# Expert layer of a two-layer transformer on one Trainium2 core: early down weights, the last two groups of slots added by one-hot products, and the last batch scaled by VectorE

## The chip, the cores and the metric

The kernel runs on one core of a Trainium2 chip. The metric is the device time in microseconds (us) of one execution. The kernel before took 1477.53 us (median of three runs, 1477.40 to 1481.35). Every row below comes from one more execution of it, taken with the profiler; times in rows are microseconds from the start of its span.

## The reference, cut to what matters

Two layers, each an attention and a feed-forward part with a residual and a layer norm behind each. The input is 4 batches of 512 tokens, 256 wide. The change lies in the last part, a mixture of 64 experts:

```python
def _moe_infer(x, gate_w, w_gate, w_up, w_down):      # x: 2048 tokens x 256
    scores = softmax(x @ gate_w.T)                    # 64 experts
    topk_w, topk_i = top_k(scores, 6)
    # each expert takes its first 32 tokens (CAP = 32), in order of token
    g = einsum('ech,ehi->eci', buf, w_gate)           # 256 -> 176
    u = einsum('ech,ehi->eci', buf, w_up)
    y = einsum('eci,eih->ech', silu(g) * u, w_down)   # 176 -> 256
    return (y[flat_i, slot] * (flat_w * valid)[:, None]).reshape(T, K, H).sum(axis=1)
shared = silu(x @ sw_gate) * (x @ sw_up) @ sw_down    # a shared expert, all tokens
x = layernorm(x + moe + shared)
```

All data are fp32.

## The kernel before, in words

Engines run their own instruction lists and meet at semaphores; the order on each engine is written out by hand. Until about 1290 us the kernel does both attentions and the first feed-forward part. Then comes the expert layer:

- Tokens. `rows4` (VectorE) writes the normed rows of batch b to `rows[b]`; ScalarE stores them with their scores to DRAM (`store_rows`), once as `rows_dram` and once, the rows alone, as the start of `sums_dram`. `choose`, `list_tokens`, `merge_lists` pick each expert's 32 tokens (VectorE).
- Groups. 64 experts x 32 slots are 16 groups of 128 slots (4 experts each). GpSimd gathers the 128 rows of each group by an indirect DMA (L717).
- Weights. Each group needs 1408 KB of gate and up weights (`load_hidden`, L460) and 704 KB of down weights (`load_down`, L466, or L1064 from ScalarE's queue for groups 6 to 15). A ring of six buffers holds them (`eg`, `ed`; `RING`). SyncE (SP) issues the loads in order, each behind a wait that says its buffer is free.
- For each group s TensorE does `turn_hidden(s)` (L2266), `gate_up(s + 1)` (L2258), `rows_of(s + 2)` (L2247), `down(s)` (L2275); in some rounds also parts of the shared expert of batches 2 and 3 (`gate_up4`, `down4_products`, L2198). ScalarE copies and scales (`y_in`, L1069); VectorE multiplies (`hidden_rows`, L1641).
- Sums. Two slots of a group, or of the two groups of a pair, can belong to one token. `sum_repeats(h)` adds them by products with 0/1 matrices (`same`, `cross`), VectorE copies the sums out (`summed_rows`, L1645), and GpSimd adds the two groups' rows to `sums_dram` by two accumulating indirect DMAs (L724). A pair's scatters wait for the landing of the pair before, since both may add to one row. Pair 7 is groups 14 and 15.
- End. After all 16 scatters SP loads the sums batch by batch (`fin`, L491). VectorE adds the shared expert's rows (`last_statistics`, L1677) and takes mean and variance (L1407 to L1413), GpSimd the root (`root16`, L636), VectorE the shift (`last_norm`, L1684), ScalarE scales (L1096), SP stores a batch (L495).

## Time and profile before

| | |
|---|---|
| three timed runs | 1477.53 us median, 1477.40 to 1481.35 |
| the profiled execution | 1473.92 us, its span 1472.1 us |
| mean granted TensorE clock | 0.983 |
| busy: TensorE, its weight loads, VectorE, ScalarE, GpSimd | 95%, 76%, 64%, 39%, 38% |
| HBM read and written | 66.22 MB, 9.21 MB |

The profiled execution's 1473.92 us hold the span and 1.82 us around it. Shares of busy time are a mean over stages with different limits; for this change only the last 180 us of the span count, and in them which wait ends last.

### The profile page before, as it was taken

The numbers are of one execution on the slowest core, as the hardware profiler recorded it, in microseconds if no ns is written. First come the engines' busy times: TensorE is split into PE (matmuls) and PEld (weight loads), VectorE is DVE, ScalarE is ACT, GpSimd is POOL, SyncE is SP. The second block draws the span as 40 slices with busy tenths as digits, with TensorE's granted clock in tenths as the row PEclk, the third lists the DMA queues.
The fourth block names the chain that finished last, engine by engine and source line by source line (L and its number), as shares of the span: only waits on it lengthen the run. The fifth ranks groups of instructions, "written<-read, shape, count | busy, mean of one in ns | idle before, by whom it ended". The sixth has DMA issues, their size and how long they took to land.

```text
span 1472.1 us, 23873 instructions
## 1 busy us (share of the span) xinstructions
PE 1396.1 (95%) x8118; PEld 1114.2 (76%) x8118; DVE 934.9 (64%) x2158; ACT 579.7 (39%) x1459; POOL 555.5 (38%) x483
## 2 busy tenths in 40 slices
PE   8999999999999999999999999999999999998990
PEld 7777777777777777777777788888888888875650
DVE  5777777777877777874443457547647647885113
ACT  4444444444444444551221144334334333352322
POOL 3655555555555555400113023513423422204223
PEclk9999999999999999999999999999999999999986
DMA  5000000000002100020000020020020001479984
GB/s 182 1 11 1 12 0 11 0 11 0 11 0 63 11 0 0 14 62 11 1 0 0 1 80 8 12 76 8 9 78 7 7 15 40 126 254 311 277 235 128
DMA packets 68221, 76.39 MB, mean 52 GB/s; under 512 B 14205, under 2 KB 55445, under 8 KB 68149
## 3 DMA queue, kind: packets, MB, share of 16 engines
q1 hardware_dynamic: 56517, 58.36, 13.4%
q10 hardware_dynamic: 8560, 12.36, 2.7%
q0 software_dynamic: 3072, 4.72, 1.6%
q8 instruction: 44, 0.72, 0.2%
q14 instruction: 28, 0.23, 0.0%
HBM read 66.22 MB, written 9.21 MB: 51 GB/s over the span
## 4 chain that ended last, share of the span: by engine, by line
PE 81%; DVE 7%; POOL 4%; ACT 3%; issue 2%; DMA 2%; SPq 1%; POOLq 0%; ACTq 0%; DVEq 0%
PE ps L1699 37%; PE ps L1838 9%; PE ps L1812 7%; PE ps L1800 5%; PE ps L1875 4%; PE ps L1966 4%; PE ps L1805 2%; PE ps L2198 2%; PE ps L2049 2%; PE ps L2258 1%; DMA wo<-in_L_attn_wo_dram 1%; PE ps L2039 1%; PE ps L2275 1%; PE ps L1840 1%; PE ps L1802 1%
## 5 line engine op out<-in xcount | busy, mean ns | idle before, releaser
L808 ACT ACTIVATE probs<-ps,nm 128x128 f32<-128x128 f32 (+3 forms) x256 | 134.0, 526 | 150.1 <-DVE nm L1189 150.1
L650 POOL TENSOR_TENSOR qk<-q,ksb 128x512 f32<-128x512 f32 x64 | 83.5, 1304 | 285.4 <-ACT q L903 212.3
L1838 PE MATMUL ps<-kT,qT 128*128 128x128 f32 (+3 forms) x512 | 174.5, 449 | 4.4 <-ACT probs L808 4.4
L1104 DVE TENSOR_TENSOR pT_low<-ps,pT 128x384 fp32r<-128x384 f32 (+2 forms) x256 | 99.6, 451 | 123.1 <-ACT pT L734 121.9
L1121 DVE TENSOR_TENSOR prod<-ps,rope_sb 128x1024 f32<-128x1024 f32 x128 | 150.2, 1215 | 7.4 <-PE ps L1699 7.4
L734 ACT ACTIVATE pT<-ps 128x384 fp32r<-128x384 f32 (+2 forms) x256 | 84.7, 416 | 152.4 <-PE ps L1875 152.4
L524 POOL TENSOR_TENSOR qT<-prod 64x512 f32<-64x512 f32 x64 | 81.2, 1269 | 167.4 <-DVE prod L1121 128.8
L1812 PE MATMUL ps<-U,oT 128*128 (+1 forms) x512 | 124.5, 386 | 0.0
L524 POOL TENSOR_TENSOR kT<-prod 64x512 f32<-64x512 f32 x64 | 81.4, 1272 | 108.7 <-DVE prod L1121 106.2
L1189 DVE TENSOR_REDUCE nm<-ps 128x1 f32<-128x128 f32 (+3 forms) x256 | 113.6, 484 | 9.3 <-PE ps L1840 9.3
L1246 DVE SCALAR_TENSOR_TENSOR acc<-ps,rinv,acc 128x256 f32<-128x256 f32 x256 | 109.4, 478 | 11.9 <-PE ps L1812 11.9
L1812 PEld LDWEIGHTS ps<-U,oT 128*128 128x128 f32 x512 | 92.4, 190 | 30.9 <-issue 20.9
L1699 PEld LDWEIGHTS ps<-kvo,qn 128*128 128x128 f32 x768 | 100.2, 191 | 8.7 <-DVE qn L1104 4.0
L1699 PE MATMUL ps<-kvo,qn 128*128 128x256 f32 x768 | 102.4, 283 | 2.9 <-DVE qn L1104 2.9
L1699 PE MATMUL ps<-wq,x2T 128*128 128x512 f32 x384 | 99.5, 395 | 5.2 <-POOL wq L582 5.2
L1699 PE MATMUL ps<-xT,wq 128*128 128x512 f32 x384 | 100.1, 408 | 0.5 <-DVE prod L1121 0.5
L1388 DVE SCALAR_TENSOR_TENSOR k<-ps,k 128x512 fp32r<-128x512 f32 x64 | 43.9, 686 | 82.8 <-ACT k L903 82.8
L1838 PEld LDWEIGHTS ps<-kT,qT 128*128 128x128 f32 x512 | 77.4, 190 | 22.6 <-issue 14.2
L1699 PE MATMUL ps<-k,x 128*128 128x512 f32 x384 | 91.6, 394 | 0.2
L1699 PEld LDWEIGHTS ps<-wq,x2T 128*128 128x128 f32 x384 | 72.3, 189 | 21.9 <-issue 4.5
L1699 PEld LDWEIGHTS ps<-xT,wq 128*128 128x128 f32 x384 | 74.2, 194 | 15.0 <-DVE prod L1121 1.3
L1800 PEld LDWEIGHTS ps<-pT,c_tok 128*128 128x128 f32 x384 | 65.6, 188 | 26.1 <-ACT pT_end L734 20.3
(263 smaller groups left out, 2767.9 us busy)
## 6 DMA issues: line engine op xcount, KB each, us to landing
eg<-in_L_ffn_w_gate_dram SPq DMA_DIRECT2D x16, 704.0 KB
eg<-in_L_ffn_w_up_dram SPq DMA_DIRECT2D x16, 704.0 KB
ed<-in_L_ffn_w_down_dram ACTq DMA_DIRECT2D x10, 640.0 KB
ksb<-ks_dram SPq DMA_DIRECT2D x16, 256.0 KB, 3.3
ed<-in_L_ffn_w_down_dram SPq DMA_DIRECT2D x6, 640.0 KB
rows_dram<-rows ACTq DMA_DIRECT2D x4, 640.0 KB, 9.0
acc<-in_L_attn_x_dram SPq DMA_DIRECT2D x4, 512.0 KB
wq_in<-in_L_attn_wq_dram SPq DMA_DIRECT2D x8, 256.0 KB, 2.9
```

The costliest lines, as they stand in the source:

```text
L524: nc.gpsimd.tensor_tensor(dst[0:64, h, b, :], byc[r, 0, :], bys[r, 1, :], ALU.subtract).then_inc(roped, 1)
L650: nc.gpsimd.tensor_tensor(qk[:], q3[:], ksb[b % 2][:], ALU.mult).then_inc(qk_ready, 1)
L734: return nc.scalar.activation(o, i, ACT.Copy)
L808: nc.scalar.activation(probs[hh][:, off:off + (i + 1) * P], ps[:, BS + i % 2, 0:(i + 1) * P], ACT.Exp, bias=nm[:, hh, i:i + 1], accum_out= ...
L1104: return nc.vector.tensor_tensor(o, whole, hi.bitcast(F32), ALU.subtract)
L1121: nc.vector.tensor_tensor(prod[parity][w][:], ps[:, BA:BA + 2, :], rope[:, w:w + 1, :].broadcast_to([P, 2, T]), ALU.mult).then_inc(product ...
L1189: nc.vector.tensor_reduce(nm[:, hh, i:i + 1], ps[:, BS + i % 2, 0:(i + 1) * P], AX_X, ALU.max, negate=True).then_inc(negmax_ready, 1)
L1246: nc.vector.scalar_tensor_tensor(out=a, in0=ps[:, BW + i // 2, (i % 2) * D:(i % 2 + 1) * D], scalar=rinv[:, hh, i:i + 1], in1=a, op0=ALU.m ...
L1699: last = pe.matmul(o, lhs(a), rhs(c), start=start and j == 0, stop=stop and j == 2)
L1800: pe.matmul(ps[:, BO, k * P:T], c_tok[h][:, b * TPB + k, :], pT[:, k, k * P:T], start=k == 0 and h == 0, stop=False)
L1812: last = pe.matmul(ps[:, BW + i // 2, (i % 2) * D:(i % 2 + 1) * D], oT[:, i * P:(i + 1) * P], U[:, bass.ds(2 * g + n % 2, 1), :], start=Tr ...
L1838: pe.matmul(ps[:, bank, 0:(i + 1) * P], qT[:, hh, b, i * P:(i + 1) * P], kT[:, hh, b, 0:(i + 1) * P], start=True, stop=False)
```

## The change

Three things change in the expert layer.

1. Loads. The down weights of groups 3 and 2 are issued right behind group 1's, that of group 2 after a wait for `kvo_ready`. Gate and up weights of groups 2, 3 and 4 follow one another after `out3_ready`; group 4's down weights wait for batch 0's shared gate and up products (`gate4_ready`). To free their places `rows3` and one half of `x3T` of batch 0 lie elsewhere; VectorE's first `match_slots` now waits until `rows3` is stored.
2. Groups 14 and 15 are no longer scattered. GpSimd writes the numbers 0 to 1023 (`tokens`), VectorE compares them with each slot's token and so makes two 0/1 matrices of 128 slots x 2048 tokens (`onehot`), and TensorE multiplies these with the groups' outputs (`y_in`), tile by tile of 128 tokens (`last_rows`), in four pairs of PSUM banks. The shared expert's rows come into the same banks by a product with the identity (batches 1 to 3), or are added by VectorE (batch 0). SP loads the sums after 14 scatters.
3. The last batch is scaled by VectorE (`last_tiles`) and stored in two halves.

```diff
-        x3T ... enumerate(((44, 117), (109, 113), (32, 36), (48, 52)))]
-        rows ... enumerate((61, 56, 104, 85))]
+        x3T ... enumerate(((100, 117), (109, 113), (32, 36), (48, 52)))]
+        rows ... enumerate((61, 56, 104, 40))]
+        onehot = [place(f"onehot{h}", at, [P, TOK]) for h, at in enumerate((32, 76))]
+        tokens = place("tokens", 24, [P, TOK // 2])
+        SCATTERED = GROUPS - 2
+        last_banks = ((5, 6), (0, 1), (3, 4), (2, 7))
...
 # SyncE
             for s in range(2):
                 load_experts(s)
+            load_down(3)
+            sp.wait_ge(kvo_ready, 2 * BLOCKS)
+            load_down(2)
             sp.wait_ge(out3_ready, BLOCKS * PPC)
-            for s in (2, 3):
-                load_experts(s)
+            for s in (2, 3, 4):
+                load_hidden(s)
             sp.wait_ge(sw_lo, 2)
-            wait_rows(sp, 3)
-            load_experts(4)
+            sp.wait_ge(gate4_ready, FT1)
+            load_down(4)
...
-            sp.wait_ge(scattered, 16 * GROUPS)
+            sp.wait_ge(scattered, 16 * SCATTERED)
...
-            for b in range(BATCH):
+            for b in range(BATCH - 1):
                 sp.wait_ge(out_done, TPB * b + TPB)
                 sp.dma_start(out_dram[b], fin[:, b * TPB:(b + 1) * TPB, :]).then_inc(stored, 16)
+            for lo in (0, TPB // 2):
+                hi = lo + TPB // 2
+                sp.wait_ge(last_done, last_done_first + hi)
+                sp.dma_start(out_dram[BATCH - 1][:, lo:hi, :], fin[...]).then_inc(stored, 16)
...
 # GpSimd
-            for s in range(GROUPS):
+            for s in range(SCATTERED):
+                if s == 10:
+                    pool.wait_ge(gate4_ready, BATCH * FT1)
+                    nc.gpsimd.iota(tokens[:], pattern=[[1, TOK // 2]], ...).then_inc(consts4, 1)
...
 # VectorE
             dve.wait_ge(gate4_ready, 2 * FT1)
+            wait_rows(dve, 3)
             match_slots(0)
...
                 if s + 2 < GROUPS:
                     hidden_rows(s + 2)
-            summed_rows(GROUPS // 2 - 1)
+                if s == 12:
+                    dve.wait_ge(consts4, 10)
+                    dve.wait_ge(down4, 2 * BATCH)
+                    link(nc.vector.tensor_scalar(spare[:, 0:2], idxf[:, SCATTERED:GROUPS], float(-(TOK // 2)), None, ALU.add))
+                if s in (12, 13):
+                    h = s - 12
+                    settle()
+                    for half, index in enumerate((idxf[:, s + 2:s + 3], spare[:, h:h + 1])):
+                        nc.vector.tensor_scalar(onehot[h][:, half * (TOK // 2):(half + 1) * (TOK // 2)], tokens[:], index, None,
+                                                ALU.is_equal).then_inc(onehot_ready, 1)
+            def add_sums(b):
+                dve.wait_ge(sums_loaded[b], sums_loaded_first[b] + 16)
+                dve.wait_ge(y_summed, SCATTERED // 2 + b + 1)
+                for j, bank in enumerate(last_banks[b]):
+                    ...  # fin of two tiles += the bank, 128x512
+            def first_sums():     # batch 0: acc += banks, before its sums are loaded
+            def add_first_sums(): # fin += acc
+            def last_tiles():
+                b = BATCH - 1
+                dve.wait_ge(rstd_ready, 13 + b)
+                for t in range(b * TPB, b * TPB + TPB):
+                    nc.vector.tensor_scalar(fin[:, t, :], fin[:, t, :], meanvar16[:, t, 0:1], rstd16[:, t:t + 1],
+                                            ALU.subtract, ALU.mult).then_inc(last_done, 1)
+            first_sums()
+            add_first_sums()
+            statistics16(0, fin)
+            for b in range(1, BATCH):
+                add_sums(b)
+                statistics16(b, fin, lambda: last_shift(b - 1))   # the shift stands amid the four bn_stats
+            last_tiles()
...
 # TensorE
+                if s == GROUPS - 1:
+                    pe.wait_ge(shared_done, 2 * BATCH)
+                    shared_of_second(1)
                 down(s)
...
-            sum_repeats(GROUPS // 2 - 1)
+            def last_rows(b):
+                if b == 0:
+                    pe.wait_ge(hid4_ready, BATCH * FT1)
+                if b == 2:
+                    pe.wait_ge(y_copied, SCATTERED // 2)
+                if b == 0:
+                    pe.wait_ge(onehot_ready, onehot_first + 4)
+                    pe.wait_ge(y_scaled, GROUPS)
+                for i in range(TPB):
+                    o = ps[:, last_banks[b][i // 2], (i % 2) * D:(i % 2 + 1) * D]
+                    t = b * TPB + i
+                    if b >= 2:
+                        pe.matmul(o, ident[:], acc[:, t, :] if b < BATCH - 1 else shared_last[:, i, :], start=True, stop=False)
+                    for h in range(2):
+                        last = pe.matmul(o, onehot[h][:, t * P:(t + 1) * P], y_in[h][:], ...)
+                last.then_inc(y_summed, 1)
+            shared_of_second(0)
+            for b in range(BATCH):
+                last_rows(b)
```

On SyncE's queue, at the loads of groups 1 to 5 (`eg`: gate and up weights of a ring place, `ed`: its down weights), there stood:

```order
L466 DMA ed1<-in_L1_ffn_w_down_dram 8x4x512
L460 DMA eg2<-in_L1_ffn_w_gate_dram 128x4x352 [waits out3_ready]
L460 DMA eg2<-in_L1_ffn_w_up_dram 128x4x352
L466 DMA ed2<-in_L1_ffn_w_down_dram 80x4x512
L466 DMA ed2<-in_L1_ffn_w_down_dram 8x4x512
L460 DMA eg3<-in_L1_ffn_w_gate_dram 128x4x352
L460 DMA eg3<-in_L1_ffn_w_up_dram 128x4x352
L466 DMA ed3<-in_L1_ffn_w_down_dram 80x4x512
L466 DMA ed3<-in_L1_ffn_w_down_dram 8x4x512
L460 DMA eg4<-in_L1_ffn_w_gate_dram 128x4x352 [waits dn_loaded,sw_lo]
L460 DMA eg4<-in_L1_ffn_w_up_dram 128x4x352
```

and there stands now:

```order
L473 DMA ed3<-in_L1_ffn_w_down_dram 80x4x512
L473 DMA ed3<-in_L1_ffn_w_down_dram 8x4x512
L473 DMA ed2<-in_L1_ffn_w_down_dram 80x4x512 [waits kvo_ready]
L473 DMA ed2<-in_L1_ffn_w_down_dram 8x4x512
L467 DMA eg2<-in_L1_ffn_w_gate_dram 128x4x352 [waits out3_ready]
L467 DMA eg2<-in_L1_ffn_w_up_dram 128x4x352
L467 DMA eg3<-in_L1_ffn_w_gate_dram 128x4x352
L467 DMA eg3<-in_L1_ffn_w_up_dram 128x4x352
L467 DMA eg4<-in_L1_ffn_w_gate_dram 128x4x352
L467 DMA eg4<-in_L1_ffn_w_up_dram 128x4x352
L473 DMA ed4<-in_L1_ffn_w_down_dram 80x4x512 [waits gate4_ready,sw_lo]
L473 DMA ed4<-in_L1_ffn_w_down_dram 8x4x512
```

Two groups' down weights moved in front of the wait for `out3_ready`, and group 4's three loads moved from behind the wait for stored rows (`dn_loaded`) to in front of it. Group 5's loads keep their wait for `gate4_ready`.

On VectorE, around the products `hE` of groups 14 and 15 and the copies `xg` of pairs 5, 6 and 7, there stood:

```order
L1645 COPY xg<-ps 128x2x256 [waits y_summed]
L1641 TENSOR_TENSOR hE<-actE,ps 128x176 [waits hE_turned,actE_ready] x2
L1645 COPY xg<-ps 128x2x256 [waits y_summed] x2
L1677 TENSOR_TENSOR fin<-fin,acc 128x1024 [waits shared_done,wd_loaded]
L1407 BN_STATS stat<-fin 128x6 [waits dchain]
```

and there stands now:

```order
L1666 COPY xg<-ps 128x2x256 [waits y_summed]
L1662 TENSOR_TENSOR hE<-actE,ps 128x176 [waits hE_turned,actE_ready]
L1696 TENSOR_SCALAR spare<-idxf 128x2 [waits down4,consts4]
L1701 TENSOR_SCALAR onehot0<-tokens,idxf 128x1024 [waits dchain]
L1701 TENSOR_SCALAR onehot0<-tokens,spare 128x1024
L1662 TENSOR_TENSOR hE<-actE,ps 128x176 [waits hE_turned,actE_ready]
L1701 TENSOR_SCALAR onehot1<-tokens,idxf 128x1024 [waits dchain]
L1701 TENSOR_SCALAR onehot1<-tokens,spare 128x1024
L1666 COPY xg<-ps 128x2x256 [waits y_summed]
L1717 TENSOR_TENSOR acc<-acc,ps 128x512 [waits y_summed]
L1717 TENSOR_TENSOR acc<-acc,ps 128x512
L1723 TENSOR_TENSOR fin<-fin,acc 128x1024 [waits wd_loaded,dchain]
```

The four comparisons stand around the product of group 15 and in front of the copy of pair 6; the copy of pair 7 is gone.

On TensorE, behind the turn of group 15's hidden rows, there stood `down(15)` and the three products of the last pair:

```order
L2275 MATMUL ps<-ed,hET 32x256 [waits y_scaled,hET_ready]
L2275 MATMUL ps<-ed,hET 32x256 x7
L2284 MATMUL ps<-y_in,same 128x256 [waits y_copied,y_scaled]
L2285 MATMUL ps<-y_in,cross 128x256
L2286 MATMUL ps<-y_in,same 128x256
```

and there stands now (the rows for tiles of batches 2 and 3 repeat in the pattern of the last two):

```order
L2357 MATMUL ps<-acc,ident 128x512 [waits hE_ready,shared_done]
L2329 MATMUL ps<-ed,hET 32x256 [waits y_scaled,hET_ready]
L2329 MATMUL ps<-ed,hET 32x256 x7
L2357 MATMUL ps<-acc,ident 128x512 [waits hET_ready,hE_ready]
L2396 MATMUL ps<-y_in,onehot 128x256 [waits y_scaled,gw_turned,hid4_ready]
L2396 MATMUL ps<-y_in,onehot 128x256 x15
L2394 MATMUL ps<-acc,ident 128x256 [waits y_copied]
L2396 MATMUL ps<-y_in,onehot 128x256 x2
```

One product of the identity moved into the gap in front of `down(15)`, another stands behind it, and 40 products of 128x256 follow.

## Rows read from the trace of the kernel before

**Rows 1.** The chain that ended last, from pair 6's copy on: start, us, what.

```profile
1434.76 0.70 DVE xg L1645
...
1437.59 3.72 DMA sums_dram<-xg,sidx
...
1443.90 3.78 DMA sums_dram<-xg,sidx
1447.70 3.88 DMA fin<-sums_dram
...
1451.60 1.24 DVE fin L1677
...
1466.76 1.97 ACT fin L1096 x4
```

**Rows 2.** Timeline, TensorE's `gate_up`: start, us, what, [idle before <-releaser].

```profile
1366.42 1.39 PE L2258 MATMUL ps<-eg,xsT 128*32 128x352 f32 x16
...
1373.49 1.39 PE L2258 MATMUL ps<-eg,xsT 128*32 128x352 f32 x16
...
1406.29 2.57 PE L2258 MATMUL ps<-eg,xsT 128*32 128x352 f32 x16 [3.32 <-issue]
...
1417.60 1.39 PE L2258 MATMUL ps<-eg,xsT 128*32 128x352 f32 x16
...
1430.97 1.39 PE L2258 MATMUL ps<-eg,xsT 128*32 128x352 f32 x16
```

**Rows 3.** Windows: five engines' busy us, TensorE's granted clock, DMA share, GB/s.

```profile
1300.00:1304.00 4.00, 2.32 (x17) 2.08 (x17) 3.88 (x21) 1.08 (x2) 0.00 (x0) 0.84 1.08 347
1324.00:1328.00 4.00, 1.05 (x12) 0.45 (x10) 3.39 (x13) 0.60 (x1) 0.00 (x0) 1.00 0.69 208
1325.50:1333.10 7.60, 4.42 (x29) 3.44 (x30) 3.97 (x11) 0.60 (x1) 4.05 (x4) 1.00 1.02 300
1345.00:1402.00 57.00, 56.16 (x458) 34.36 (x455) 17.32 (x52) 17.76 (x44) 15.04 (x11) 1.00 1.08 289
1406.00:1416.00 10.00, 9.71 (x47) 5.43 (x48) 1.03 (x2) 0.70 (x2) 0.77 (x1) 0.53 1.08 297
1428.00:1431.00 3.00, 3.00 (x40) 1.26 (x33) 0.75 (x2) 1.38 (x4) 2.01 (x2) 1.00 0.11 5
```

**Rows 4.** Timeline of SyncE's queue: first load of groups 4 and 5.

```profile
1323.90 0.39 SPq L460 DMA_DIRECT2D eg<-in_L_ffn_w_gate_dram  x1
...
1331.47 0.39 SPq L460 DMA_DIRECT2D eg<-in_L_ffn_w_gate_dram  x1
```

**Rows 5.** Timeline of GpSimd: the first gather, then a scatter of pair 5.

```profile
1328.06 1.20 POOL L717 DMA_INDIRECT xg<-rows_dram,gidx  x1 [30.70 <-DVE gidx L1569]
...
1428.68 1.56 POOL L724 DMA_INDIRECT sums_dram<-xg,sidx  x1 [10.04 <-DVE xg L1645]
```

**Rows 6.** Timeline of all engines, the end of the span.

```profile
1432.78 0.34 DVE L1641 TENSOR_TENSOR hE<-actE,ps 128x176 f32<-128x176 f32 x1 [2.81 <-ACT actE L1057]
...
1435.86 1.07 PE L2275 MATMUL ps<-ed,hET 88*32 88x256 f32 x16 [0.92 <-ACT y_in L1069]
1436.99 0.47 ACT L1069 ACTIVATE y_in<-ps,wslot 128x256 f32<-128x256 f32 x1 [1.27 <-PE ps L2275]
...
1438.05 0.59 PE L2285 MATMUL ps<-y_in,cross 128*128 128x256 f32 x2
...
1438.48 0.59 PE L2286 MATMUL ps<-y_in,same 128*128 128x256 f32 x2
...
1461.31 1.22 DVE L1677 TENSOR_TENSOR fin<-fin,shared_last 128x1024 f32<-128x1024 f32 x1
1461.41 1.99 POOL L636 TENSOR_TENSOR rstd<-vareps,halfp 128x4 f32<-128x4 f32 x1 [1.27 <-DVE vareps L1413]
...
1464.67 1.01 POOL L636 TENSOR_TENSOR rstd<-vareps,halfp 128x4 f32<-128x4 f32 x1 [1.27 <-DVE vareps L1413]
```

**Rows 7.** Timeline of VectorE: four normed tiles of 128x256 in fp32.

```profile
1296.26 1.37 DVE L1420 TENSOR_SCALAR rows<-acc,meanvar,rstd 128x256 f32<-128x256 f32 x4
```

More of the change, by code:

```diff
@@ L1091, in _ @@
             outputs4(GROUPS - 1)
-            for b in range(BATCH):
+            for b in range(BATCH - 1):
                 act.wait_ge(shift_ready, b + 1)
@@ L1403, in add3, with statistics16 @@
                 nc.vector.tensor_tensor(a, a, ps[:, 6 + tile % 2, 0:D], ALU.add).then_inc(added3, 1)
-            def statistics16(b, source):
+            def statistics16(b, source, between=None):
                 for t in range(b * TPB, b * TPB + TPB):
+                    if between is not None and t == b * TPB + TPB // 2:
+                        between()
                     link(nc.vector.bn_stats(stat16[:, t, :], source[:, t, :]))
@@ L1681, in last_norm @@
-            def last_norm(b):
+                if s == 12:
[8 more added lines that the diff above has]
+                                                ALU.is_equal).then_inc(onehot_ready, 1)
@@ L2314, in _ @@
                     down4_products(3, s - 10)
-            sum_repeats(GROUPS // 2 - 1)
+            def last_rows(b):
[12 more added lines that the diff above has]
+                    for h in range(2):
+                        last = pe.matmul(o, onehot[h][:, t * P:(t + 1) * P], y_in[h][:], start=b == 0 and h == 0, stop=h == 1,
+                                         skip_group_check=b == 1)
+                last.then_inc(y_summed, 1)
+            shared_of_second(0)
+            for b in range(BATCH):
+                last_rows(b)
 def rope_tables():
```

41 lines of the change are left out of this document (28 added, 13 removed).

## The prediction

> **What bounds the kernel now.** I read the chain of waits from its end first [rows 1]: the reader is to see that after TensorE's last work for pair 6 nothing but a string of hand-overs is left. VectorE copies pair 6 (1434.76), GpSimd scatters it (landed 1437.59 + 3.72 = 1441.3), then scatters pair 7 (landed 1443.90 + 3.78 = 1447.7), SP loads the sums (3.88), VectorE treats four batches, ScalarE scales the last one until 1466.76 + 1.97 = 1468.73, and 3.37 us later the span ends (1472.1). That is 37 us with every compute engine mostly idle. Then the timeline of TensorE [rows 2]: its `gate_up` of group 11 idles 3.32 us in front of 1406.29, put down to "issue", with VectorE and ScalarE long done. It waits for that group's weights. The windows [rows 3] say why: from 1345 to 1402 the DMA engines are at 1.08 of their time (289 GB/s), so the weights come as fast as they can. They also show the price behind the stall: TensorE's granted clock is 0.53 from 1406 to 1416, so mostly its lower level, 1.2 GHz. From `gate_up` 11 to 12 go 1417.60 - 1406.29 = 11.31 us; the like round from group 5 to 6 (also with one `down4_products`) took 7.07. So the fall costs 4.2 us, the stall with it 7.5.
>
> **Early loads.** Three transfers of group 4 (2112 KB) and the down weights of groups 2 and 3 leave their place. Bytes are the same in all; what counts is how far ahead the saturated queue is when group 5 is asked for. SP issues group 5 at 1331.47 before [rows 4]; it waited for TensorE's `gate4_ready`, which no edit moves, so it does so again. Group 4 was asked for at 1323.90, and its first bytes came about 1.6 us later, at 1325.5: a share of 0.69 of the 4 us from 1324 to 1328 is 2.5 to 2.8 us of traffic [rows 3]. From 1325.5 to 1333.1 (when group 5's first bytes may come by the same lag) the engines moved 7.6 x 300 = 2.28 MB [rows 3]. Asked for by then were group 4's 2.16 MB and the gathers: 128 rows x 320 x 4 B = 0.164 MB each, the first at 1328.06 [rows 5], issued in 1.20 us each, three or four of them, 0.49 to 0.66 MB. So 0.37 to 0.54 MB were left over at 1333.1. With group 4 already there nothing is left over. At 300 GB/s that puts the queue ahead by 1.2 to 1.8 us, less what an idle moment before 1345 gives back. I take 1.2; the bounds are 0 and 1.8. Most of the moved 3.6 MB is worth nothing for that reason: a queue that was empty before 1323.90 anyway only gets its idle time filled, and group 5 still starts when TensorE says so.
>
> Group 11 then arrives 1.2 us earlier, the idle before its `gate_up` is 2.1 us. Whether the clock still falls is open. Gaps in the stretch 1300 to 1304 (TensorE busy 2.32 of 4.00) brought it to 0.84, larger ones from 1324 to 1328 (busy 1.05 of 4.00) did not touch it [rows 3]. I take that it falls: -1.2 us for this part. The new wait on VectorE (`rows3` stored) stands behind the wait for `gate4_ready`, hence after 1331, and SP saw those rows stored when it issued group 4 at 1323.90: nothing. Earlier queue traffic delays batch stores by at most the 0.72 MB of group 4's down weights (2.4 us at 300 GB/s), and nobody waits for them before the gathers at 1328.06.
>
> **One pair of scatters less.** SP may load the sums when pair 6 has landed. Before it did so at 1447.70, pair 6 was there at 1441.35: -6.35 us. What has to be done instead is the products, and the question is only whether they are late. TensorE: one 128x512 product in front of `down(15)`. A 128x256 one takes 1438.48 - 1438.05 = 0.43 us [rows 6], so this takes 0.86, and TensorE idled 0.92 there: hidden. `down(15)` ends 1436.93, ScalarE's `y_in` of group 15 at 1437.46, the second 128x512 product at about 1437.8. Then 8 + 8 + 12 + 12 = 40 products of 0.43: batches are done at 1441.2, 1444.7, 1449.8 and 1455.0 (1455.2 with the latency of the last). VectorE wants batch 0's while it waits for the loads, until 1445.2, and the others at 1449.1, 1452.4 and 1455.7, as worked out below. All are in time, the last by 0.5 us only.
>
> VectorE's four comparisons of 128x1024 stand between old work. Price: the nearest rows are the four 128x256 TENSOR_SCALARs, the same operation with as many elements in all, 1.37 us [rows 7], and one TENSOR_TENSOR of 128x1024, 1.22 us [rows 6]. I take 1.15 us apiece, so 2.3 per pair (bounds 1.2 and 2.8). The first pair fits between the products of groups 14 and 15 (2.81 us idle). The second starts at 1432.78 + 0.34 = 1433.12 and ends at 1435.4, where the copy of pair 6 stood ready at 1434.76: +0.6 us for the copy, the scatters of pair 6 and everything after (0 to 1.1). The rows show fp32 TENSOR_SCALAR to be no faster per element than TENSOR_TENSOR. The Trainium skill, page "VectorE: DVE Perf Modes", section on the perf-mode tier table, says otherwise: with one fp32 source in SBUF this operation runs at twice the rate of a TENSOR_TENSOR. By that rule the pair would take 1.2 us, the copy would not be late, and the sum below would be 0.6 us less (a rival below); I go by the rows. GpSimd's list of 1024 numbers falls into its 10.04 us idle time in front of 1428.68 [rows 5]: nothing.
>
> **The batches at the end.** VectorE takes (1461.31 - 1451.60) / 3 = 3.24 us per batch [rows 1, 6]. Batch 0 starts at 1451.60 - 6.35 + 0.6 = 1445.85. For batches 1 to 3 one add of 128x1024 becomes two of 128x512 with a PSUM source; a 128x512 copy from PSUM is 0.70, two overlap a little: 1.27 against 1.22, +0.05 each (0 to 0.2). The shift now stands amid the four `bn_stats`: in batch 3 that is +0.1. It waits there for GpSimd's root of the batch before, some 2 us after that batch's variance. The root took 1.99 us beside VectorE's add of two SBUF tensors, and 1.01 us alone [rows 6]; the add has one PSUM source now, so I take 1.01 and no wait. With 1.99 it would cost 0.2 us a batch, 0.6 in all. The Trainium skill ("GPSIMD Engine Reference", specifications) says that GpSimd shares its SBUF interfaces with VectorE and contends with it when an instruction has two SBUF inputs. By it these roots should shrink to about 1 us, which is the value taken.
>
> Batch 3 before: root done at 1464.67 + 1.01 = 1465.68, ScalarE done at 1468.73, since it was still at batch 2: 3.05 us. Now four TENSOR_SCALARs of 128x256 on VectorE, 1.37 [rows 7]: -1.7 us. The last store is half as large, but stands behind batch 2's and its own first half: nothing (-0.7 to 0). So 3.37 us from the last value to the end stay.
>
> **Sum.** -1.2 (queue) - 6.35 (pair 7) + 0.6 (comparisons) + 0.15 + 0.1 (adds, shift) - 1.7 (last batch) = -8.4 us. The profiled execution would take 1473.92 - 8.4 = 1465.5, its span 1463.7. The timed median is 3.6 above that execution, so I forecast 1477.53 - 8.4 = 1469.1 us. A difference under 0.3% (4.4 us) counts as no change here.
>
> **Rivals.**
> - The clock does not fall. For it: the idle shrinks to 2.1 us, and 1324 to 1328 shows longer gaps without a fall. Against: 1300 to 1304. It would give the 4.2 us back, but not freely: `gate_up` of group 15 ran at 1430.97, and the DMA engines are done by about 1428 (0.11 from 1428 to 1431), so TensorE could be at most 2.9 us earlier, plus the queue's 1.2. That is -4.1 instead of -1.2: 1466.2 us. Chance 24%.
> - The early loads give nothing, as an idle moment of the queue before 1345 eats the lead: stall and fall stay as they are: 1470.3 us. Chance 14%.
> - The products become the bound. They have 0.5 us to spare; if a product took 0.47 us instead of 0.43, 40 would take 1.6 us more, and the end moves by 1.1: 1470.2. If the clock falls once in this stretch for a few us, 2 or 3 us are lost, 1471 to 1472. Chance 8%.
> - The comparisons cost nothing: at half the time of the TENSOR_TENSOR row the second pair ends at 1433.12 + 1.2 = 1434.3, before 1434.76. Against it are the four tiles in 1.37 us. 1468.5 us. Chance 8%.
> - Slower than before: TensorE runs the whole stretch of products at 1.2 GHz. 17.2 us become 34.4, batch 3 is ready at 1472.3, and from there 9.2 us lead to the end (1464.9 without the queue's 1.2, less 1455.7): span 1481.5, less 1.2 is 1480.3, 8.2 over before, timed 1485.7. It costs from the moment that over 0.5 us is lost, and eats the whole gain of 8.4 when TensorE spends some 18 us of the stretch at 1.2 GHz. Against it: gaps up to 0.92 us in front of it leave no long idle time, and the products stand back to back. Chance 3%.
> - The change doesn't do what it says: a wait keeps the sums' load behind something else (products of batch 0, `onehot`), or weights arrive in another order and starve TensorE twice. A second stall with its fall costs 7.5 us: 1476.6, no change. Chance 5%.
>
> The forecast itself has 38%. Its own range, with the clock's fall, is 1467.5 to 1471.5. Range for eight in ten: 1464.5 to 1474.0; below it lie cases where both the clock and the comparisons turn out well, above it the last two rivals. Faster by over 0.3% (under 1473.1): the forecast and the first four rivals, 92%, less the part of them that errs by 4 us: 0.86. Within 0.3%: 0.10. Slower: 0.04.
>
> **What would show it.** Right: SP's load of the sums within 0.1 us of pair 6's landing, 5.5 to 6 us earlier than before against the end of TensorE's last `down`; two comparisons of 1.2 us in front of pair 6's copy, and that copy 0.6 us behind its `y_summed`; roots of 1.0 us; VectorE's adds of batches 2 and 3 without idle time in front of them; DMA share near 0 around 1325 to 1331 but `gate_up` of group 11 still idle for about 2 us, with a granted clock under 0.8 behind it. Wrong: that `gate_up` without a stall; VectorE idle in front of batch 3's add (the products bound); the sum load late against the scatters.

## The result, and the profile after

The changed kernel took 1470.95 us (median of five runs, 1469.85 to 1473.80) and the kernel before 1479.11 us beside it (1477.40 to 1481.35). The ratio is 0.9948, with a 95% interval from 0.9937 to 0.9959: 7.7 us less (6.1 to 9.3). I had forecast 1469.1 us and -8.4. The profiled execution of the changed kernel took 1473.80 us (span 1472.0, mean clock 0.989), 2.9 us above its own median, and hardly less than the profiled one of before (1473.92 us). So read side by side the two profiles show no gain at all. The timeline of ScalarE in the changed kernel says where it went:

```profile
1337.15 0.60 ACT L753 ACTIVATE acc<-ps 128x512 f32<-128x512 f32 x1 [4.35 <-PE ps L2252]
1350.00 0.60 ACT L753 ACTIVATE acc<-ps 128x512 f32<-128x512 f32 x1 [12.26 <-remote]
```

In front of the second of two copies of one stage ScalarE is idle for 12.26 us. TensorE's products for it ended by 1339.9, so it was ready for 10.1 of them; "remote" is the profile's word for a release that it can't name, and its chain of waits calls it so:

```profile
1337.74 12.23 another core or an unknown queue
```

The first `gate_up` stands at 1351.56 for that reason, in the profile of before at 1340.53. TensorE's timeline in the changed kernel, groups 0, 5, 11, 12, 13 and 15, is the answer to [rows 2]:

```profile
1351.56 2.58 PE L2312 MATMUL ps<-eg,xsT 128*32 128x352 f32 x16
...
1379.47 1.39 PE L2312 MATMUL ps<-eg,xsT 128*32 128x352 f32 x16
...
1415.95 1.39 PE L2312 MATMUL ps<-eg,xsT 128*32 128x352 f32 x16
1423.02 1.39 PE L2312 MATMUL ps<-eg,xsT 128*32 128x352 f32 x16
1429.97 1.39 PE L2312 MATMUL ps<-eg,xsT 128*32 128x352 f32 x16 [1.11 <-issue]
...
1438.51 1.39 PE L2312 MATMUL ps<-eg,xsT 128*32 128x352 f32 x16 [0.43 <-issue]
```

There is no stall of 3.32 us and no slow `gate_up` at group 11. TensorE comes 11.0 us later at group 0 and 13.1 at group 5, since behind the pause the clock is at its lower level for two groups (2.58 us instead of 1.39); at group 15, 7.5 us of that are left. The weights came later too: SP asked for those of group 6 at 1354.19 instead of 1341.98. But by then all gathers had landed, while before they still shared the engines with group 6. That the stall is gone for this reason isn't shown. The end of the chain answers to [rows 1]:

```profile
1442.30 0.70 DVE xg L1666
...
1445.14 3.81 DMA sums_dram<-xg,sidx
...
1448.96 3.86 DMA fin<-sums_dram
```

SP loads the sums when pair 6 has landed, 1445.14 + 3.81. From pair 6's copy to the end are 1472.0 - 1442.30 = 29.7 us, where before they were 1472.1 - 1434.76 = 37.3. Since the pause hides all else in this profile, the terms below are read from a second profile of the same kernel (after_again), which has no pause.

### The profile page after: what moved, and what is told of

The parts are those of the page before. It is cut to its first block, busy times and chain, and to the rows that moved or that the text cites. A ratio compares the mean times of both kernels' runs of the same rounds, so it can differ in the third digit from the quotient of the medians.

```text
span 1472.0 us, 24039 instructions
## 1 busy us (share of the span) xinstructions
PE 1414.7 (96%) x8196; PEld 1129.8 (77%) x8196; DVE 939.4 (64%) x2170; ACT 577.1 (39%) x1455; POOL 550.9 (37%) x482
## 4 chain that ended last, share of the span: by engine, by line
PE 81%; DVE 7%; POOL 4%; ACT 2%; issue 2%; DMA 2%; another core or an unknown queue 1%; SPq 1%; POOLq 0%; ACTq 0%; DVEq 0%
PE ps L1753 38%; PE ps L1892 9%; PE ps L1866 7%; PE ps L1854 5%; PE ps L1929 4%; PE ps L2020 4%; PE ps L1859 2%; PE ps L2103 2%; PE ps L2312 2%; DMA wo<-in_L_attn_wo_dram 1%; PE ps L2093 1%; PE ps L2329 1%; PE ps L2252 1%; PE ps L1894 1%; PE ps L1856 1%
```

## The experiments

Kernels with the same time of before ran on one chip, beside the kernel before. Medians in us; "pause" is ScalarE's stop of 12 us in the profile.

| kernel | median (runs) | before | ratio, 95% interval | profiled | pause |
|---|---|---|---|---|---|
| after_again | 1466.40 (6) | 1474.66 | 0.9948 [0.9934, 0.9963] | 1465.54 | no |
| loads_only | 1474.49 (12) | 1474.66 | 0.9999 [0.9989, 1.0010] | 1476.09 | no |
| tail_only | 1466.38 (6) | 1474.66 | 0.9948 [0.9933, 0.9962] | 1465.83 | no |
| act_last | 1466.60 (6) | 1474.66 | 0.9947 [0.9932, 0.9962] | 1466.68 | no |
| less_bytes | 1472.01 (6) | 1480.16 | 0.9940 [0.9917, 0.9963] | 1472.53 | yes |
| filled_stall | 1475.47 (12) | 1480.16 | 0.9966 [0.9952, 0.9979] | 1474.50 | yes |
| cmp_pieces | 1472.70 (10) | 1480.16 | 0.9954 [0.9934, 0.9974] | 1471.42 | yes |
| more_products | 1472.97 (10) | 1480.16 | 0.9952 [0.9937, 0.9967] | 1472.74 | yes |
| before_again | 1479.53 (8) | 1479.93 | 0.9993 [0.9978, 1.0007] | 1481.10 | yes |
| gathers_split | 1466.67 (4) | 1479.93 | 0.9915 [0.9900, 0.9931] | 1466.82 | shorter stops |
| before_vector_last | 1480.22 (9) | 1479.93 | 1.0014 [1.0001, 1.0027] | 1477.69 | yes |
| gathers_fours | 1468.60 (6) | 1480.84 | 0.9920 [0.9905, 0.9935] | 1469.00 | one of 3 us |

### after_again: the changed kernel once more

> The changed kernel once more. Its profiled execution (1473.8 us) stood 2.9 us over its own median, and showed a ScalarE copy (acc, group of batch 1) only at 1350.00, 12.3 us idle in front of it and nothing in the profile to wait for, and so the first gate_up at 1351.56 instead of 1340.5. Theory A (the pause is a chance event of single executions, not made by the change): another profile has no such pause or a much shorter one, the first gate_up stands near 1340, and gate_up of group 11 idles about 2 us with the clock falling behind it, as I had predicted; execution near 1466 to 1471. Theory B (the early loads make the pause, and the time that the DMA engines gain in it is what takes the stall of group 11 away): the pause is there again, 8 to 10 us, and group 11 has no stall. Median: 1470 to 1471.5 with either.

Theory A. TensorE's timeline, `gate_up` of groups 0, 11, 12, 13 and 15, and two windows (columns as in [rows 3]):

```profile
1340.49 1.39 PE L2312 MATMUL ps<-eg,xsT 128*32 128x352 f32 x16
...
1403.02 1.39 PE L2312 MATMUL ps<-eg,xsT 128*32 128x352 f32 x16 [0.17 <-issue]
1415.00 2.58 PE L2312 MATMUL ps<-eg,xsT 128*32 128x352 f32 x16 [4.85 <-issue]
1422.66 1.39 PE L2312 MATMUL ps<-eg,xsT 128*32 128x352 f32 x16
...
1430.27 1.39 PE L2312 MATMUL ps<-eg,xsT 128*32 128x352 f32 x16
```

```profile
1325.50:1333.10 7.60, 5.96 (x30) 4.44 (x30) 2.62 (x6) 0.60 (x1) 5.17 (x6) 0.78 0.36 95
...
1413.00:1419.00 6.00, 4.00 (x27) 1.39 (x31) 0.34 (x1) 0.70 (x2) 1.62 (x2) 0.50 1.11 299
```

The stall hasn't gone. It stands one group later and is larger (4.85 + 0.17 us against 3.32), with the clock at its lower level behind it. The idle time of the DMA engines that I foresaw is there (0.36 where [rows 3] have 1.02).

### loads_only, tail_only: each half of the change alone

loads_only is the kernel before with the edits of SyncE's loads, the two places and VectorE's wait for `rows3`. tail_only is the changed kernel with this undone:

```diff
-            load_down(3)
-            sp.wait_ge(kvo_ready, 2 * BLOCKS)
-            load_down(2)
             sp.wait_ge(out3_ready, BLOCKS * PPC)
-            for s in (2, 3, 4):
-                load_hidden(s)
+            for s in (2, 3):
+                load_experts(s)
             sp.wait_ge(sw_lo, 2)
-            sp.wait_ge(gate4_ready, FT1)
-            load_down(4)
+            wait_rows(sp, 3)
+            load_experts(4)
```

> The kernel before with the early loads alone (all 16 groups scattered, last batch by ScalarE). Prediction on record: -1.2 us (bounds -1.8 to 0), copy of pair 6 to the end still 37.3 us. Theory A: 0 to -2 us against before, gate_up 11 still idles 2 to 3 us. Theory B (the early loads make a 10 us pause in front of group 0, which takes the stall and the clock fall of 7.5 us away): the pause and no stall, +0 to +3 us against before.

> The changed kernel with the loads in the order of before (one-hot products and VectorE's last batch stay). From pair 6's copy to the end 29.7 us as in the changed kernel against 37.3 of before, and the comparisons cost nothing in front of that copy: -7.6 us against before with theory A if the loads give 0, then equal to the changed kernel; if the loads give the -1.2 of my prediction it is 1.2 slower than the changed kernel, -6.5. Theory B: no pause before group 0, stall of 3.3 us at group 11 with the clock fall, -7.6.

Measured: the loads alone 0.9999, everything else alone 0.9948, like the whole change. `gate_up` of groups 0, 11 and 15 in loads_only:

```profile
1342.26 1.39 PE L2262 MATMUL ps<-eg,xsT 128*32 128x352 f32 x16
...
1411.27 2.58 PE L2262 MATMUL ps<-eg,xsT 128*32 128x352 f32 x16 [6.56 <-issue]
...
1433.07 1.39 PE L2262 MATMUL ps<-eg,xsT 128*32 128x352 f32 x16
```

and of groups 0, 11 and 12 in tail_only:

```profile
1339.00 1.39 PE L2309 MATMUL ps<-eg,xsT 128*32 128x352 f32 x16
...
1402.41 1.39 PE L2309 MATMUL ps<-eg,xsT 128*32 128x352 f32 x16 [1.06 <-issue]
1413.65 1.59 PE L2309 MATMUL ps<-eg,xsT 128*32 128x352 f32 x16 [4.11 <-issue]
```

Where `gate_up` 12 waits, its start is the arrival of its weights. Counted from `gate_up` 0 this is 1413.65 - 1339.00 = 74.65 us with the old loads and 1415.00 - 1340.49 = 74.51 with the early ones: a lead of 0.14 us, not 1.2 (act_last, with the early loads too: 74.44). The reason is how far the queue was with the old loads when group 5 was asked for. SyncE's first loads of groups 4 and 5 in tail_only, and its window from 1.6 us behind the one to 1.6 us behind the other:

```profile
1320.45 0.39 SPq L467 DMA_DIRECT2D eg<-in_L_ffn_w_gate_dram  x1
...
1329.94 0.38 SPq L467 DMA_DIRECT2D eg<-in_L_ffn_w_gate_dram  x1
```

```profile
1322.05:1331.57 9.52, 6.02 (x29) 4.52 (x30) 4.29 (x11) 0.86 (x2) 5.12 (x6) 0.82 1.00 293
```

SP asked for group 4 9.49 us in front of group 5. It did so in before_again (1321.92 and 1331.41) and before_vector_last (1321.24 and 1330.73) too; only in the profile that the prediction was made from was it 7.57 us [rows 4]. With the prediction's own working tail_only moved 9.52 x 293 = 2.79 MB. Asked for were group 4's 2.16 MB and four gathers, 0.66 MB, so 0.03 MB were left over, 0.1 us. The old loads leave as little in the queue as the early ones. The moment at which group 6 is asked for shows it again, in windows of before, of after_again, and of tail_only at the same place (its `gate_up` 0 stands 1.49 us earlier):

```profile
1342.00:1343.00 1.00, 0.27 (x2) 0.24 (x2) 0.66 (x2) 0.30 (x1) 0.90 (x1) 1.00 1.15 278
```

```profile
1342.00:1343.00 1.00, 0.31 (x2) 0.24 (x2) 0.67 (x2) 0.27 (x1) 0.69 (x2) 1.00 0.85 128
```

```profile
1340.51:1341.51 1.00, 0.31 (x2) 0.24 (x2) 0.67 (x2) 0.27 (x1) 0.69 (x2) 1.00 0.96 128
```

SP asks for group 6 at 1341.98 before and at 1341.95 after: its place in the ring comes free with `gate_up` 0, which no edit moves. In the first profile of before group 5's weights still flow then. With the early loads they have landed and only gathers flow (128 GB/s), and with the old loads in tail_only it is the same.

tail_only's chain also shows a wait that no theory had. Pair 5's second scatter, what waits for it, and a window in front of it:

```profile
1429.77 5.03 DMA sums_dram<-xg,sidx
...
1435.53 1.56 POOL sums_dram L740
```

```profile
1426.00:1430.00 4.00, 4.00 (x43) 2.11 (x41) 1.80 (x5) 1.45 (x4) 1.79 (x2) 1.00 0.00 0
```

It lands after 5.03 us instead of 3.8, pair 6's scatters wait for it, and 0.6 us are lost (7.2 us from pair 6's copy to the load of the sums, 6.7 in after_again). In less_bytes (landing 5.88) and more_products (6.07) 1.3 us are; filled_stall (5.05) and gathers_fours (5.15) show it too. It isn't the weights: the last of them had landed, and the DMA engines stood idle from 1426 to 1430. In all five GpSimd issued it beside VectorE's first pair of comparisons and took 1.72 us instead of 1.56; so it did in after_again, act_last and gathers_split (1.72 each), where nobody had to wait for its landing. No kernel without comparisons shows it. Whether they make it late stays open.

### act_last, before_vector_last: who scales the last batch

act_last undoes `last_tiles` and the store in halves in the changed kernel; before_vector_last puts both into the kernel before.

```diff
-            for b in range(BATCH - 1):
+            for b in range(BATCH):
                 act.wait_ge(shift_ready, b + 1)
...
-            last_tiles()
+            last_shift(BATCH - 1)
```

> The changed kernel with the last batch scaled by ScalarE behind a shift by VectorE and stored whole, as before. Prediction on record: VectorE's last batch is worth 1.7 us (root to last value 1.37 against 3.05). So +1.7 us against the changed kernel, -6.0 against before. Rival: ScalarE is free earlier now (its third batch ended 1467.1, the last could start at 1467.6 behind the shift), so only the 0.7 us between 2.07 and 1.38 and the shift of 0.15 are won: +0.8 us. What the two halves of the store give comes on top: 0 to 0.7 us.

> The kernel before with the last batch scaled by VectorE and stored in two halves, nothing else. My prediction took 1.7 us for that (3.05 us from the end of the root to ScalarE's last value, against 1.37). In the changed kernel undoing it cost 0.97 us in the profile (act_last). Theory A (the other 0.7 us came from ScalarE being late behind roots of 2 us, and those became 1 us by another edit): here the whole 1.7 us shows, from pair 6's copy to the end 35.6 us instead of 37.3. Theory B (1.0 us in either kernel): 36.3 us.

act_last's last root and ScalarE's last four tiles:

```profile
1458.28 1.01 POOL L646 TENSOR_TENSOR rstd<-vareps,halfp 128x4 f32<-128x4 f32 x1 [2.51 <-DVE vareps L1430]
1459.52 2.07 ACT L1111 ACTIVATE fin<-fin,shift,rstd 128x256 f32<-128x256 f32 x4 [0.49 <-DVE shift L1725]
```

From the root's end (1459.29) to the last value are 2.30 us, where VectorE takes 1.42 in after_again. ScalarE isn't late any more, so VectorE is worth 0.9 us, 1.0 with the store (30.7 us from pair 6's copy to the end, against 29.7): the rival of that expectation. In times it can't be seen (0.9947 against 0.9948).

Why ScalarE was late before is seen at VectorE's shift of batch 2, in before and in after_again:

```profile
1464.50 0.15 DVE L1684 SCALAR_TENSOR_TENSOR shift<-meanvar,rstd 128x4 f32<-128x4 f32 x1
```

```profile
1456.65 0.15 DVE L1729 SCALAR_TENSOR_TENSOR shift<-meanvar,rstd 128x4 f32<-128x4 f32 x1
```

Before, the root that this shift needs had ended at 1461.41 + 1.99 = 1463.40 [rows 6], and VectorE came to the shift 1.1 us later, behind all `bn_stats` of batch 3. So the long root delayed nothing there. The shift stood 1.18 us in front of the last root's end (1465.68), and ScalarE needs 2.07 us for a batch. Now it stands amid the `bn_stats`, 2.51 us in front of that end (1459.16), and ScalarE is free in time. before_vector_last keeps the shift's old place. Its ScalarE at batch 2, VectorE's last batch and SP's last stores:

```profile
1469.01 2.07 ACT L1100 ACTIVATE fin<-fin,shift,rstd 128x256 f32<-128x256 f32 x4 [1.18 <-DVE shift L1688]
1470.03 1.38 DVE L1697 TENSOR_SCALAR fin<-fin,meanvar,rstd 128x256 f32<-128x256 f32 x4 [1.06 <-POOL rstd L640]
1471.52 1.54 SPq L499 DMA_DIRECT2D out_dram<-fin  x2
```

The last value is 1.64 us earlier against the root, but ScalarE ends batch 2 only at 1471.08, SP issues stores in order, and the last ones start at 1471.52. From pair 6's copy to the end: 1475.9 - 1438.96 = 36.9 us, 0.5 less than in before_again (1479.3 - 1441.83 = 37.5). Both theories fell. Timed it is no gain (1.0014, 1.0001 to 1.0027).

### cmp_pieces: what a comparison costs

```diff
-    nc.vector.tensor_scalar(onehot[h][...1024...], tokens[:], index, None, ALU.is_equal).then_inc(onehot_ready, 1)
+    for q in range(4):   # 256 numbers each
+        piece = nc.vector.tensor_scalar(onehot[h][...], tokens[:, q * 256:(q + 1) * 256], index, None, ALU.is_equal)
+    piece.then_inc(onehot_ready, 1)
```

> The changed kernel with each comparison of 128x1024 cut into four of 128x256. My prediction priced a 128x1024 comparison at 1.15 us by the four 128x256 TENSOR_SCALARs in 1.37 us; the profile shows 0.75 (0.68 apart). Theory A (an instruction has a fixed share of about 0.2 us, so that the small ones say nothing of the rate per element): 0.34 us apart, 1.37 us for four, the pair 2.75, the copy of pair 6 ready 1.0 to 1.3 us later than now, that much slower: +1.1 us. Theory B (the rows normed at 1296 had another reason, two scalars from SBUF or other work beside them): 0.17 to 0.2 us apiece, nothing changes.

VectorE in cmp_pieces, and below it in after_again, up to pair 6's copy:

```profile
1438.08 1.14 DVE L1702 TENSOR_SCALAR onehot<-tokens,idxf 128x256 f32<-128x256 f32 x4
1439.13 1.14 DVE L1702 TENSOR_SCALAR onehot<-tokens,spare 128x256 f32<-128x256 f32 x4
1440.18 0.68 DVE L1666 COPY xg<-ps 128x512 f32<-128x512 f32 x1
```

```profile
1432.33 0.75 DVE L1701 TENSOR_SCALAR onehot<-tokens,idxf 128x1024 f32<-128x1024 f32 x1
1433.00 0.75 DVE L1701 TENSOR_SCALAR onehot<-tokens,spare 128x1024 f32<-128x1024 f32 x1
1434.06 0.69 DVE L1666 COPY xg<-ps 128x512 f32<-128x512 f32 x1 [0.31 <-PE ps L2340]
```

Four pieces follow each other in 1.05 us, one of 1024 in 0.67: a share of (1.05 - 0.67) / 3 = 0.13 us belongs to each instruction. Theory A in kind, with a smaller share than it said. The rest of the 1.37 us of [rows 7] I put down to that form (two operations with a number each); no run takes it apart. The copy came 4.15 us behind `gate_up` 15 instead of 3.79: 0.36 us. The timed runs can't tell this (0.9954) nor more_products (0.9952) from the changed kernel.

### more_products: are the products the bound

```diff
                 if b == 2:
                     pe.wait_ge(y_copied, SCATTERED // 2)
+                if b == 3:
+                    for _ in range(4):
+                        pe.matmul(ps[:, last_banks[3][0], 0:D], ident[:], shared_last[:, 0, :], start=True, stop=True, ...)
```

> The changed kernel with four more products of 128x256 (never read) in front of batch 3's, 1.73 us. Theory A (the products are already the bound by 0.1 us: in the last profile batch 3's add started at 1454.66, 0.1 us behind their end and 0.03 after VectorE was ready by 0.1): +1.7 us from pair 6's copy to the end. Theory B (0.5 us of slack, as in my prediction): +1.2 us. The profile's add of batch 3 shows which: TensorE named in front of it with 1.7 or 1.2 us.

VectorE's add of batch 3 in more_products, and in after_again:

```profile
1461.83 1.28 DVE L1709 TENSOR_TENSOR fin<-fin,ps 128x512 f32<-128x512 f32 x2 [0.44 <-PE ps L2400]
```

```profile
1454.66 1.28 DVE L1709 TENSOR_TENSOR fin<-fin,ps 128x512 f32<-128x512 f32 x2
```

From pair 6's copy to the end it takes 1471.0 - 1439.51 = 31.5 us, 1.75 more than after_again, as much as four products (1.73). The late scatter hides 1.3 of it; without that all 1.75 would stand before the add. So theory A: no slack. In after_again TensorE's last product ended at 1454.56, and the add follows the start of the TENSOR_SCALAR in front of it (L1434) by 0.20 us, by 0.08 in the batches before. Batches took 3.19, 3.32 and 3.45 us there, 3.19, 3.33 and 3.32 in tail_only, where the sums came later: 0.13 us lost to the products.

### filled_stall, less_bytes: the stall, and the lead

```diff
+                if s == 11:      # filled_stall, TensorE
+                    pe.wait_ge(hid4_ready, BATCH * FT1)
+                    for _ in range(4):
+                        pe.matmul(ps[:, 5, :], ident[:], acc[:, 0:2, :]..., start=True, stop=True, ...)
```

```diff
                 for w, name in enumerate(("gate", "up")):
+                    if s == 8 and w == 1:      # less_bytes, SyncE: 16 of 128 partitions
+                        sp.dma_start(eg[i][0:16, :, w, :, :]..., io["L1_ffn_w_" + name]...[0:16, 4 * s:4 * s + 4, :])
+                        continue
```

> The changed kernel with four more products of 128x512 (identity, into a free bank, never read; 0.86 us each, 3.4 us) on TensorE in front of gate_up of group 12, where three profiles of one-hot kernels showed 3.8 to 4.9 us idle and a clock of 0.5 for 6.8 us. Theory A (the idle time brings the clock down, and the fall costs 1.9 us, as group 12 to 13 took 7.66 us against 5.77 at full clock): idle under 1.5 us, no fall, -1 to -2 us. Theory B (the clock falls all the same, or the weights of groups 13 to 15 end the stream so late that a faster TensorE waits for them): 0. Where the stall stands at group 11 instead, they cost up to 3.4 us.

> The changed kernel with seven eighths of group 8's up weights not loaded (0.62 MB less in the queue; group 8's products use what group 2 left there, so the sums are not the reference's). It gives all groups from 9 on a real lead of 0.62 MB / 278 GB/s = 2.2 us in the saturated queue, and asks what a lead is worth. Theory A (the early loads were worth nothing because group 6 can only be asked for when gate_up 0 has freed its place, so that they make no lead; a real lead counts): the 4.9 us idle at gate_up 12 becomes 2.7 us, the last gate_up stands about 2.2 us earlier against gate_up 0 than in the changed kernel (89.8 us), median -2 us (-4 where the clock does not fall). Theory B (the early loads did make a lead of 1.2 us, and a lead is worth nothing at the end, since the clock falls anyway or another transfer ends later): 0 to -0.5 us.

Both ran beside the pause, where there is no stall to fill or to shorten, and say little. In filled_stall `gate_up` 11 and 12 stand 1425.47 - 1414.96 = 10.5 us apart instead of 7.07: all 3.44 us (0.0023) are paid; timed it is 0.0018 worse than the changed kernel, with intervals that overlap. In less_bytes the waits in front of groups 13 to 15 (1.9 us in the first profile) are gone, but filled_stall has none either and more_products 0.23 us, with all bytes loaded; 1.3 us are lost at the scatters, and 0.9940 can't be told from 0.9948. What a real lead is worth, and what keeping the clock up would give, stays open.

### before_again, gathers_split, gathers_fours: the pause

> The kernel before, once more. Five of nine profiles of kernels with the early loads show ScalarE's last copy acc of batch 1 only at 1348 to 1350 (12 us idle, nothing named), 0.3 us behind the landing of the last gather; the other four show it at 1338 to 1339. The kernel before was timed at 1474.7 us beside the second kind and at 1479 to 1480 beside the first. Theory A (the pause belongs to the chip or the placement, not to the change): beside a before of 1477 us or more, the kernel before has the pause too, gate_up 0 near 1350 and no stall at group 11; beside 1475 or less there is none. Theory B (the early loads bring the pause where the chip allows it): no pause here in either case, gate_up 0 near 1340.5.

The kernel before has the pause too, so the change doesn't make it:

```profile
1349.19 0.60 ACT L734 ACTIVATE acc<-ps 128x512 f32<-128x512 f32 x1 [12.18 <-remote]
```

Seven profiles show it, all beside a before of 1479 us or more; the four beside 1474.7, and the first one of before (1473.92), show none. ScalarE goes on about 1 us after the last gather's data. Windows of cmp_pieces, where it goes on at 1347.53 (the column before the last is the DMA share); in the first profile the share falls to 0.00 at 1349, and it goes on at 1350.00:

```profile
1346.00:1347.00 1.00, 0.00 (x0) 0.00 (x0) 0.00 (x0) 0.00 (x0) 0.00 (x0) 0.50 0.22 87
1347.00:1348.00 1.00, 0.00 (x0) 0.00 (x0) 0.00 (x0) 0.47 (x1) 0.00 (x0) 0.50 0.00 0
```

```diff
             for s in range(GROUPS):
+                if s == 4:       # gathers_split
+                    pool.wait_ge(gu4_ready, 1)
                 nc.gpsimd.indirect_dma_start(out=xg[:, s, :], ...)
```

> The changed kernel with GpSimd waiting for gate_up of group 0 before it issues gathers 4 to 15. Theory A (where the pause occurs, ScalarE waits until the last gather has landed, 0.3 us behind it in the profiles): the pause ends with gather 3, so gate_up 0 stands near 1341 instead of 1350; then the stall of the weights comes back at group 11 or 12 (5 us and the clock), so that -4 us of the 8 to 9 remain against the changed kernel. Where there is no pause: 0, or +0.5 us, as the gathers now share the engines with group 6's weights, -0.5 as group 5's have them for themselves. Theory B (the pause is bound to a place in ScalarE's program, as a code load would be, and not to the gathers): the pause is as long as before, 0 us.

```diff
+                if q:                # gathers_fours, a run of four: q = 0 to 2, and 3 behind four scatters
+                    pool.wait_ge(gu4_ready, (1, 4, 8)[q - 1])
+                for s in range(4 * q, 4 * q + 4): ...
-                if s in (1, 2, 3):   # VectorE
-                    weigh(s)
+                if s in (1, 6, 10):
+                    weigh((1, 6, 10).index(s) + 1)
```

> The changed kernel with the gathers in four runs of four: behind the stored rows, behind gate_up 0, behind gate_up 3, and behind gate_up 7 (there after four scatters); VectorE reads the weights of quarters 2 and 3 at groups 6 and 10 instead of 2 and 3, since it would wait for the gathers otherwise. gathers_split took the 8.5 us pause away in front of group 0 (gate_up 0 at 1339.9), but 12 gathers in a row then stood beside two shorter stops of ScalarE, 5.8 us (1346.5 to 1352.3) and 5.2 us, at other places of its program. Theory A (long runs of gathers stop ScalarE on the chips that show the pause; four in a row never did): no stop at all, gate_up 0 at 1339.9, the stall of the weights and its clock fall come back at group 12 as in the undisturbed profile of the changed kernel, gate_up 0 to 15 takes 89.8 us instead of 91.7, ratio 0.990. Theory B (a stop comes with any gather beside saturated weight loads): stops of some us at each run of four, 1 to 5 us slower than gathers_split. On a chip without the pause: ratio as the changed kernel's, 0.9948, by either.

gathers_split has the lowest ratio of the study, 0.9915 of before; its interval ends at 0.9931, the changed kernel's begins at 0.9937. Its ScalarE:

```profile
1352.30 0.38 ACT L755 ACTIVATE hET<-ps 88x256 f32<-88x256 f32 x1 [7.40 <-issue]
...
1358.81 0.32 ACT L1078 ACTIVATE actE<-ps 128x176 f32<-128x176 f32 x1 [5.20 <-remote]
```

`gate_up` 0 stood at 1339.86 and nothing stopped ScalarE in front of it; 12 gathers in a row then stood beside two stops at other places of its program. So the pause isn't bound to one place in the program; a load of instructions that stands behind gathers, now at one place and now at another, was not tested. But the first of these stops ended at 1352.30 with three gathers still to be issued, so "until the last has landed" isn't the rule either. With runs of four (gathers_fours) a single stop of 3.05 us is left, and then the weights' stall and its clock fall come back, 1.08 and 4.19 us:

```profile
1388.56 0.32 ACT L1084 ACTIVATE actE<-ps 128x176 f32<-128x176 f32 x1 [3.05 <-remote]
```

```profile
1415.78 2.58 PE L2320 MATMUL ps<-eg,xsT 128*32 128x352 f32 x16 [4.19 <-issue]
```

From `gate_up` 0 to 15 it takes 94.1 us, gathers_split 91.7: fewer stops, but no time won (0.9920 and 0.9915, intervals overlap). Neither theory holds as written. What ScalarE waits for is not settled, and how both kernels do where there is no pause wasn't measured.

## Why the prediction was right, point by point

The forecast for the profiled execution was 1465.5 us; after_again, which like the profile of before has no pause, took 1465.54. The timed difference is -7.7 us, forecast were -8.4. That the sum meets the execution within 0.1 us is luck, since it holds better than its terms:

- **Early loads, -1.2.** This step failed in size: 0. loads_only gives 0.9999 (-1.6 to +1.5 us), the arrival of group 12 moved 0.14 us. "So 0.37 to 0.54 MB were left over at 1333.1" held for one execution, in which group 4 was asked for 1.9 us late; in tail_only 0.03 MB were left over with the old loads. "With group 4 already there nothing is left over" is true then, but nothing was left over without it either. The rival "the early loads give nothing" was right in its outcome; its reason, an idle moment before 1345, isn't needed. From `gate_up` 0 to 15 the kernels without a pause took 90.4 and 91.2 us with the old loads (before, tail_only), 89.8, 91.0 and 90.8 with the early ones (after_again, act_last, loads_only): I take the 0.66 us between after_again and before for scatter of single executions.
- **The clock falls.** Right, though the stall is at group 12. The price of 4.2 us is that of one execution: at group 12 the fall costs 1.9 us in after_again (group 12 to 13 in 7.66 us, and 5.76 before), 3.2 in tail_only and act_last, 4.1 in gathers_fours, and at group 11 in loads_only 1.4. Stall and fall together took 7.5 us before, 6.9 in after_again, 8.3 in tail_only, 8.1 in act_last, 7.9 in loads_only and 9.4 in gathers_fours. Why the stall stands at 11 in the two kernels without one-hot products and without a pause, and at 12 in the four with them that have a stall, I don't know.
- **Comparisons, +0.6.** Wrong: 0 in front of that copy. They take 0.67 us apiece, not 1.15; `gate_up` 15 to pair 6's copy is 3.79 us in both kernels. My nearest rows were four instructions for one, and each carries a share of its own (0.13 us in cmp_pieces). The rule of the Trainium skill, "VectorE: DVE Perf Modes", perf-mode tier table, which I had set aside, says that with one fp32 source in SBUF this operation takes about half the time of a TENSOR_TENSOR. Measured were 0.67 against 1.22 us, so the trace agrees with it. Should the comparisons be what makes pair 5's scatter late, they cost 0.6 to 1.3 us there in some executions; the forecast had no such wait.
- **One pair less, -6.35.** Copy to load of sums 12.94 us before, 6.66 after: -6.28. Right.
- **Adds and shift, +0.25.** From the first add to the last 9.71 us before, 9.96 after; from the last add to the end of the last root, where batch 3's part of the shift stands, 4.37 and 4.50. That is +0.38, and 0.13 of it is the products: without them the term is right.
- **Products, 0.43 us apiece, slack 0.5.** Price right (40 of them end at 1454.56, 17.4 us after they began), slack wrong: none. The 0.6 us that I gave VectorE for the comparisons were the slack; they cost it nothing, so it met the products' end 0.1 us too soon.
- **Roots of 1.01 us.** Right: 1.04, 1.00, 1.01 and 1.01. Before, it was 1.99 [rows 6] beside VectorE's add of two SBUF tensors, and the adds read PSUM now. The Trainium skill ("GPSIMD Engine Reference", specifications) says that GpSimd shares its SBUF interfaces with VectorE and contends with instructions that have two SBUF inputs. The trace agrees.
- **Last batch, -1.7.** Root to last value 3.05 us before, 1.42 after: -1.63, as a difference of the two kernels. As a price of the edit it was wrong: VectorE instead of ScalarE is worth 0.9 of it, the other 0.75 came with the shift's new place, which let ScalarE end batch 2 in time (act_last, before_vector_last). Under "The batches at the end" I gave that place a cost of 0.1 us and no gain.
- **The end.** Last value to end 3.37 before, 3.22 after.

Two errors cancelled. The loads gave nothing where I took -1.2 us, but 0.7 us came back in that execution by scatter; the comparisons cost nothing where I took +0.6. So the copy of pair 6 was forecast 0.6 us earlier and came 0.70 earlier. All of the change's gain lies behind that copy, 7.6 us in the first profile, which is also what the timed runs show (7.7, and tail_only has it without the loads). "The timed median is 3.6 above that execution" was an offset that I took as it stood. Most likely it is the pause, which the profile of before lacks and before_again, timed at 1479.53, has; timed runs carry no trace, so this isn't shown. All timed runs that the forecast rests on and is compared with have about 1477 to 1481 us for before, so the offset cancelled, by luck too.

## What to carry to other kernels

A transfer that is issued earlier is worth something only if some of it was still outstanding when the next one was asked for; work that out from more than one profile, since one execution here had 0.4 MB left over and three others next to nothing. Price an edit by the difference of two chains, not by the engine's time alone: the last batch on VectorE was worth 0.9 or 0.5 us, depending on how late the others were, and a shift moved by a few instructions gave the other 0.75. When a profile and the timed runs disagree by a few us, look for a stop that one of them has and the other lacks before comparing two profiles.

## What the runs showed of the hardware that I had not expected

- ScalarE stood still for 12 us with nothing named to wait for (ready for about 10 of them), in all seven profiles of kernels with 16 gathers in a row that were taken beside a before of 1479 us or more, and in none beside 1475. The two kinds of chips differ by 4.6 to 4.9 us in the time (1479.5 against 1474.7 for before, 1470.95 against 1466.40 for the changed kernel). That the pause makes this difference isn't shown, as no chip was seen with and without it; behind it the clock is at its lower level for two groups, and most of the weights' stall is gone. 12 gathers later in the program moved it, runs of four left 3 us.
- A scatter of 128 rows landed 3.8 us after its issue with idle DMA engines, but in five profiles one of them took 5.0 to 6.1 us, with the weights all landed; GpSimd had issued it beside VectorE's comparisons.
- A 128x1024 TENSOR_SCALAR with one number per row took 0.67 us, cut in four 1.05 us.
